# Two-layer transformer block, one core: one order of products for the gated layer, its last rows stored by tiles, up biases prepared by VectorE, and stage exits without a barrier where there is nothing to clear

## The reference, cut to what matters

```python
xn = layernorm(x)
x1 = x + attention(xn) + experts(xn)          # layer 0
zn = layernorm(x1)
out = x1 + lightning(zn) + gated(zn)          # layer 1

def experts(x):                               # two experts, every token takes one
    e0 = argmax(softmax(x @ Wg.T)) == 0
    out0 = gelu(x @ W0a.T + b0a) @ W0b.T + b0b
    out1 = relu(x @ W1a.T + b1a) @ W1b.T + b1b
    return where(e0, out0, out1)

def gated(x):                                 # ternary weights q(w), hidden width 1408
    return (sigmoid(x @ q(w1).T) * (x @ q(w2).T)) @ q(w3).T
```

## Time and profile before

| | us |
|---|---|
| three executions | 1728.63, 1733.5, 1733.7 |
| the profiled execution's own time | 1733.02 |
| its span, first to last instruction | 1731.2 |
| expert stage, first SyncE issue to the last add | 888.01 to 1122.3 |
| gated stage, first matmul to the end of the span | 1476.76 to 1731.2 |
| mean granted TensorE clock, share of full | 0.955 |

### The profile page before, as it was taken

How to read it: one execution, slowest core, us unless ns; L and a number is a source line. 1 busy time by engine, 2 the same in 40 slices (tenths; PEclk the granted TensorE clock), 3 DMA queues, 4 the chain that set the end, 5 groups by cost and what they waited for, 6 DMA issues and landing times. The chain is left out here.

```text
span 1731.2 us, 22070 instructions
## 1 busy us (share of the span) xinstructions
PE 1556.5 (90%) x7890; PEld 1080.1 (62%) x7890; DVE 989.4 (57%) x1698; ACT 603.2 (35%) x1137; POOL 647.9 (37%) x530
## 2 busy tenths in 40 slices
PE   5998769999999999996979999839999996999997
PEld 4886434444545555543757777737777774788886
DVE  7764857778877888762435555445654445222232
ACT  3221225555555555554212122144424222222221
POOL 4000033376788677784336666523120201000000
PEclk9998879999999999998989999959999997999999
DMA  6876503645545375224741211153030105320210
GB/s 229 264 232 205 118 4 86 128 104 103 129 119 113 78 180 116 57 87 132 242 140 55 67 56 58 52 186 128 1 122 1 50 31 152 116 98 1 98 49 25
DMA packets 103257, 182.28 MB, mean 105 GB/s; under 512 B 29018, under 2 KB 45290, under 8 KB 101274
## 3 DMA queue, kind: packets, MB, share of 16 engines
q1 hardware_dynamic: 85636, 121.39, 25.6%
q0 software_dynamic: 13648, 51.61, 10.0%
q10 hardware_dynamic: 3866, 7.87, 1.4%
HBM read 118.83 MB, written 62.02 MB: 104 GB/s over the span
## 5 line engine op out<-in xcount | busy, mean ns | idle before, releaser
L999 ACT ACTIVATE att_probs<-att_ring 128x512 f32<-128x512 f32 (+3 forms) x640 | 298.8, 537 | 295.5 <-DVE att_ring L1036 154.5
L1027 DVE TENSOR_REDUCE att_maxes<-att_ring 128x2 f32<-128x1024 f32 (+7 forms) x366 | 338.7, 946 | 68.2 <-PE att_ring L921 58.0
L956 PE MATMUL att_outp<-att_probs,att_vs 128*64 128x512 f32 (+3 forms) x1280 | 276.1, 553 | 0.3 <-ACT att_att L982 0.3
L956 PEld LDWEIGHTS att_outp<-att_probs,att_vs 128*64 128x64 f32 x1280 | 79.6, 139 | 122.0 <-issue 70.8
L942 PE MATMUL att_ring<-route_wah,route_wbh 102*128 102x512 f32 (+2 forms) x320 | 106.1, 408 | 13.4 <-ACT att_probs L999 7.3
L921 PE MATMUL att_ring<-route_wbh,route_wah 100*128 100x512 f32 (+2 forms) x320 | 103.8, 406 | 14.7 <-PEq L57 6.4
L921 PE MATMUL att_ring<-moew_wbl,moew_wal 100*128 100x512 f32 (+2 forms) x320 | 98.7, 384 | 17.2 <-ACT att_probs L999 9.0
L1685 DVE TENSOR_TENSOR glu_hid<-glu_sig,glu_u 128x512 f32<-128x512 f32 x44 | 30.2, 687 | 139.0 <-ACT glu_sig L1663 139.0
L1700 POOL DMA_DIRECT2D out<-glu_y x4 | 3.1, 787 | 278.2 <-DVE glu_y L1691 278.2
L942 PEld LDWEIGHTS att_ring<-route_wah,route_wbh 102*128 102x128 f32 x320 | 55.5, 194 | 76.1 <-issue 44.3
L942 PE MATMUL att_ring<-moew_wal,moew_wbl 102*128 102x512 f32 (+2 forms) x320 | 100.4, 399 | 2.4 <-DVE att_maxes L1027 2.3
(11 more groups left out here) (270 smaller groups left out, 3516.0 us busy)
## 6 DMA issues: line engine op xcount, KB each, us to landing
att_q_raw<-in_w POOLq DMA_DIRECT2D x48, 352.0 KB, 4.1
w_ternary<-att_q_out POOLq DMA_DIRECT2D x24, 352.0 KB, 2.7
tail_up<-w_ternary SPq DMA_DIRECT2D x22, 256.0 KB, 4.9
xn<-qkv_x SPq DMA_DIRECT2D x4, 1024.0 KB, 7.8
q_hi<-qkv_hi SPq DMA_DIRECT2D x16, 256.0 KB, 3.9
q_lo<-qkv_lo SPq DMA_DIRECT2D x16, 256.0 KB, 4.5
k_hi<-qkv_hi SPq DMA_DIRECT2D x16, 256.0 KB, 2.9
k_lo<-qkv_lo SPq DMA_DIRECT2D x16, 256.0 KB, 3.9
```

Source lines behind the costliest of these rows:

```text
L956: last = pe.matmul(outp[v_cols(h), off:CH], vs[p % 2][:, kt, v_cols(h)], probs[:, g % 4, h, off:CH], start=kt == 0, stop=kt == TT * (c + 1 ...
L999: act.activation(probs[:, g % 4, h, off:CH], ring[:, rg.banks["score", g][h], off:CH], ACT.Exp).then_inc(exped, 1)
L1027: last = dve.tensor_reduce(maxes[:, hs, t, g:g + 1], banks[:, :, 0:width], AX.X, ALU.max)
```

## The change

Four edits. An exit without semaphores neither clears nor waits at a barrier, and `up_in` moves from `Kept` into the `lin` stage, where SyncE waits for it as its last act; so `tail` has no semaphore either. In the expert stage `ba` has a semaphore of its own and VectorE subtracts in it; GpSimd waits for the other two tables and keeps their two operations. In the gated stage the loops over chunk and step become one loop over 44 steps, so that the first two up products of a chunk stand between the last down products of the one before; the sigmoid waits for `u1_made`, signalled behind the eighth matmul; VectorE's chunk-end add comes one step into the next chunk. In the last down product each token tile signals by itself, VectorE adds it (128x512) and SyncE stores it (256 KB).

```diff
@@ class Stage
     def __exit__(self, *a):
         self.stack.__exit__(*a)
-        self.nc.clear_and_free_semaphores(self.sems)
-        self.nc.all_engine_barrier()
+        if self.sems:
+            self.nc.clear_and_free_semaphores(self.sems)
+            self.nc.all_engine_barrier()
@@ experts_stage, SyncE
-            for dst, src in ((ba, ba_d), (bb, bb_d), (bo, bo_d)):
+            sp.dma_start(ba[:], ba_d).then_inc(ba_in, 16)
+            for dst, src in ((bb, bb_d), (bo, bo_d)):
                 sp.dma_start(dst[:], src).then_inc(b_in, 16)
@@ experts_stage, VectorE
             x_low(0)
-            dve.wait_ge(b_ready, 3)
+            dve.wait_ge(ba_in, 16)
+            dve.tensor_tensor(ba[:, 0, :], ba[:, 0, :], ba[:, 1, :], ALU.subtract).then_inc(ba_ready, 1)
+            dve.wait_ge(ba_ready, 1)
             select(0)
...
                 mix(0, half)
+            dve.wait_ge(b_ready, 2)
             down_bias(0)
@@ experts_stage, GpSimd
-            pool.wait_ge(b_in, 3 * 16)
-            for t in (ba, bb):
-                pool.tensor_tensor(t[:, 0, :], t[:, 0, :], t[:, 1, :], ALU.subtract).then_inc(b_ready, 1)
-            pool.wait_ge(b_ready, 2)
+            pool.wait_ge(b_in, 2 * 16)
+            pool.tensor_tensor(bb[:, 0, :], bb[:, 0, :], bb[:, 1, :], ALU.subtract).then_inc(b_ready, 1)
+            pool.wait_ge(b_ready, 1)
             pool.tensor_tensor(bb[:, 1, :], bb[:, 1, :], bo[:], ALU.add).then_inc(b_ready, 1)
@@ lightning_stage, SyncE
             for f in range(GT):
-                kept.load(sp, up_d, f)
+                kept.load(sp, up_d, f, up_in)
             sp.wait_ge(z_stored, (NCH - 1) * 32)
+            sp.wait_ge(up_in, GT * 32)
@@ glu_stage, SyncE, behind its loop
+            for t in range(TT):
+                sp.wait_ge(tile_added, t + 1)
+                sp.dma_start(rows_of(out_d, GLU_CHUNKS[NCH - 1])[:, t, :], y[:, t, :]).then_inc(tile_stored, 16)
+            sp.wait_ge(tile_stored, TT * 16)
@@ glu_stage, TensorE (the loop before is in the listing above)
+            def up_product(n):
+                c, f = divmod(n, GT)
+                if f == 0 and c:
+                    pe.wait_ge(x_in[c % 2], (c + 1) // 2 * 32)
+                pe.wait_ge(hid_ready, n + 1)
+                for w, u, made in ((w1, u1, u1_made), (w2, u2, upped)):
...
+                    last.then_inc(made, 1)
+
+            def down_product(n):
+                c, f = divmod(n, GT)
+                if f == 0:
+                    pe.wait_ge(added, c + 1)
+                if c == 0:
                     pe.wait_ge(down_in[load_of[f]], 16)
+                pe.wait_ge(lo_ready, n + 3)
+                for t in range(TT):
...
+                    if n == NF - 1:
+                        last.then_inc(tile_made, 1)
+                if n < NF - 1:
                     last.then_inc(downed, 1)
+            up_product(0)
+            up_product(1)
+            for n in range(NF):
+                down_product(n)
+                if n + 2 < NF:
+                    up_product(n + 2)
@@ glu_stage, ScalarE
+            for n in range(NF):
+                act.wait_ge(u1_made, n + 1)
+                act.wait_ge(hid_ready, n + 1)
+                act.activation(sig[:, n % 2, :], u1[:, n % 2, :], ACT.Sigmoid).then_inc(sig_ready, 1)
+                act.wait_ge(hid_ready, n + 3)
+                act.wait_ge(downed, n - 1 + LEAD)
+                act.activation(hh[:, n % 2, :], hid[:, n % 2, :], ACT.Copy).then_inc(hi_ready, 1)
@@ glu_stage, VectorE
+            def finish(c):
+                dve.wait_ge(y_free, c + 1)
+                if c:
+                    dve.wait_ge(r_in, c * 16)
+                if c + 1 < NCH:
+                    dve.wait_ge(downed, c * GT + GT + LEAD)
+                    dve.tensor_tensor(y[:], resid[:], down[:], ALU.add).then_inc(added, 1)
...
+                for t in range(TT):
+                    dve.wait_ge(tile_made, t + 1)
+                    dve.tensor_tensor(y[:, t, :], resid[:, t, :], down[:, t, :], ALU.add).then_inc(tile_added, 1)
...
+            for n in range(NF):
+                dve.wait_ge(upped, n + 1)
+                dve.wait_ge(sig_ready, n + 1)
...
+                if n and n % GT == 0:
+                    finish(n // GT - 1)
+            finish(NCH - 1)
@@ glu_stage, GpSimd
-            for c in range(NCH):
+            for c in range(NCH - 1):
```

More of the change, by code:

```diff
@@ L1300, in experts_stage @@
         up, down = st.ps("up", [P, 2, CH]), st.ps("down", [P, 2, D])
-        b_in, b_ready = st.sem("b_in"), st.sem("b_ready")
+        ba_in, b_in, ba_ready, b_ready = (st.sem(n) for n in ("ba_in", "b_in", "ba_ready", "b_ready"))
         gathered, fetched, stored = ([st.sem(f"{n}{i}") for i in range(k)]
@@ L1545, in __init__ @@
         self.up = [st.sb(f"up{i}", [P, GT, KT, P], F32R) for i in range(2)]
-        self.up_in = st.sem("up_in")
         self.xh, self.xl = st.sb("xh", [P, KT, CH], F32R), st.sb("xl", [P, KT, CH], F32R)
@@ L1558, in spare, with load @@
         return self.up[i][:, 2 * KT + j]
-    def load(self, eng, w_d, f):
+    def load(self, eng, w_d, f, arrived):
         for w, src in zip(self.up, w_d):
             eng.dma_start(w[:, f].bitcast(F32), src[:, f * P:(f + 1) * P].rearrange("(k p) n -> p k n", p=P)
-                          ).then_inc(self.up_in, 16)
+                          ).then_inc(arrived, 16)
 GLU_CHUNKS = [NCH - 1] + list(range(NCH - 1))
@@ L1584, in glu_stage @@
         x_in, r_in = [st.sem(f"x_in{i}") for i in range(2)], st.sem("r_in")
-        upped, sig_ready, hid_ready = st.sem("upped"), st.sem("sig_ready"), st.sem("hid_ready")
+        u1_made, upped, sig_ready, hid_ready = (st.sem(n) for n in ("u1_made", "upped", "sig_ready", "hid_ready"))
         hi_ready, lo_ready, downed = st.sem("hi_ready"), st.sem("lo_ready"), st.sem("downed")
+        tile_made, tile_added, tile_stored = st.sem("tile_made"), st.sem("tile_added"), st.sem("tile_stored")
         added, y_ready, stored, y_free = st.sem("added"), st.sem("y_ready"), st.sem("stored"), st.sem("y_free")
         block = st.block()
-        LEAD = 2 * GT
+        LEAD, NF = 2 * GT, NCH * GT
         def load_down(eng, i):
@@ L1614, in _ @@
             pe.sem_inc(downed, LEAD)
-            for c in range(NCH):
[L1616 to L1629, removed]
-                    pe.wait_ge(down_in[load_of[f]], 16)
[L1631 to L1635, removed]
-                    last.then_inc(downed, 1)
[L1638 to L1646, removed]
@@ new lines, in up_product @@
+            def up_product(n):
[4 more added lines that the diff above has]
+                for w, u, made in ((w1, u1, u1_made), (w2, u2, upped)):
+                    for k in range(KT):
+                        pe.matmul(u[:, n % 2, :], w[:, f, k, :], xh[c % 2][:, k, :], start=k == 0, stop=False)
+                        last = pe.matmul(u[:, n % 2, :], w[:, f, k, :], xl[c % 2][:, k, :], start=False, stop=k == KT - 1)
+                    last.then_inc(made, 1)
@@ new lines, in down_product @@
+            def down_product(n):
[3 more added lines that the diff above has]
+                if c == 0:
+                    pe.wait_ge(down_in[load_of[f]], 16)
+                pe.wait_ge(lo_ready, n + 3)
+                for t in range(TT):
+                    s = slice(t * P, (t + 1) * P)
+                    pe.matmul(down[:, t, :], hh[:, n % 2, s], w3[:, f, :], start=f == 0, stop=False)
+                    last = pe.matmul(down[:, t, :], hl[:, n % 2, s], w3[:, f, :], start=False, stop=f == GT - 1)
+                    if n == NF - 1:
+                        last.then_inc(tile_made, 1)
+                if n < NF - 1:
+                    last.then_inc(downed, 1)
@@ L1666, in _ @@
         @block.vector
         def _(dve):
+            def finish(c):
[5 more added lines that the diff above has]
+                    dve.tensor_tensor(y[:], resid[:], down[:], ALU.add).then_inc(added, 1)
+                    dve.wait_ge(added, c + 2)
+                    dve.sem_inc(y_ready, 1)
+                    return
+                for t in range(TT):
+                    dve.wait_ge(tile_made, t + 1)
+                    dve.tensor_tensor(y[:, t, :], resid[:, t, :], down[:, t, :], ALU.add).then_inc(tile_added, 1)
@@ L1671, in _ @@
             dve.sem_inc(y_ready, 1)
[L1672 to L1693, removed]
+            for n in range(NF):
+                dve.wait_ge(upped, n + 1)
+                dve.wait_ge(sig_ready, n + 1)
+                dve.wait_ge(lo_ready, n + 1)
+                dve.tensor_tensor(hid[:, n % 2, :], sig[:, n % 2, :], u2[:, n % 2, :], ALU.mult).then_inc(hid_ready, 1)
+                dve.wait_ge(hi_ready, n + 1)
+                dve.tensor_tensor(hl[:, n % 2, :], hid[:, n % 2, :], hh[:, n % 2, :].bitcast(F32),
+                                  ALU.subtract).then_inc(lo_ready, 1)
+                if n and n % GT == 0:
+                    finish(n // GT - 1)
+            finish(NCH - 1)
         @block.gpsimd
```

(2 more changed lines are left out.)

## The result

The changed kernel takes 1722.9 us (median of five, 1714.9 to 1725.8) against 1733.7 (median of five, 1728.6 to 1736.9): ratio 0.9921, 95% interval 0.9898 to 0.9944, so it is faster, by 0.6 to 1.0%. The forecast was 1721.3. The profiled execution took 1725.83 us with a span of 1724.0.

The account below looks back on a forecast made before the run. TensorE, busy 90% of the span, was taken as the bound, leaving gaps, clock and stage ends. Terms 4.0 + 4.2 + 1.3 + 2.4 = 11.9 off 1733.02 gave 1721.1, forecast as 1721.3 after splitting the offset to the median; range 1717.0 to 1726.5.

Parts of the forecast that it names:

- Chunk ends: Gated stage: next chunk's up products cover TensorE's wait and restart at three boundaries of 1.33 us, -4.0 us.
- The end: After the last up product: sigmoid off the path 0.63, tile adds 0.84, SyncE's tile stores 2.3, exit 0.4; together -4.2 us.
- Barriers: Stage exits: three empty barriers after the experts at 0.3 us each and one at the end at 0.4; -1.3 us.
- Experts: Opening of the expert stage: GpSimd loses its 2.40 us bias subtraction, so ReLU and second `mix` come earlier; -2.4 us.
- the third: Rival: experts' opening gives 4.5 us instead of 2.4, clock staying full after a shorter gap, ReLU faster; 1719.0, chance 0.08.
- the fourth rival: Slower: TensorE's clock stays at half in the experts' first tiles, 12 us a tile; 1739 at one and a half, chance 0.03.
- The first rival: Small terms pay half: last stores queue, giving back 2.1 us, and the experts' opening gives 0.5; 1725.1, chance 0.13.

Follow-up runs that it names:

- bias_only: Kernel before with only the `ba` semaphore and VectorE's bias subtraction added; it took 3.1 us off the experts.
- order_only: Kernel before with only the single order of products, sigmoid still behind the whole up product; gated stage 237.2 us against 241.2.
- add_twice: Changed kernel with the chunk-end add of 128x2048 done twice; gated stage 4.7 us more than 237.2.
- one_store: Changed kernel with the four tile adds but one 1 MB store by SyncE; landing 4.3 us, end 11.2 us long against 9.1 to 9.2.
- select_late: Changed kernel with `select(1)` moved behind the two mixes; expert stage 1.2 us longer, longest ReLU 2.02 us in place of 3.0.
- bb_on_vector: Changed kernel with both operations on `bb` moved from GpSimd to VectorE; 1716.7 us, ratio 0.9903 to the kernel before.

## Why the prediction was right

- **The sum, -11.9**: at equal clock the touched stretches gave -13.5 to -13.7. In the profile the gated stage's opening at half clock took 1.6 of it back, which nobody had forecast. That the sum was met to the tenth is luck; the mechanisms are shown one by one, each at its term or a little over it.
- **Chunk ends, -4.0**: measured -4.0 with the clock alike on both sides. The profile's -2.4 is this less the half-clock opening.
- **The end, -4.2 and 0.4 for its barrier**: measured -5.6. Gate signal -0.7 (0.6 forecast). From the last down product's start to the last add's end 3.4 us (3.7), since the four adds took 2.48 together where 2.82 was reckoned. Store 2.3 from add to landing (2.7). The exit from landing to the last instruction 0.9 (1.1), 1.1 less than before. Each term a little too careful, all the same way.
- **Barriers, -0.9 after the experts**: -1.0. The moved wait for the weights cost nothing visible: of lightning's 1.1 us more, 0.7 and 0.9 also stand in bias_only (346.1) and order_only (346.3), which have it not, while add_twice and one_store have it and took 344.3. TensorE's gap ahead of the gated stage is 2.0 us with it and 2.1 to 2.3 without.
- **Experts, -2.4**: -2.9 to -3.1. The path was named rightly; the size of one thing on it was not. The prediction let the two gathers keep their length, but the first took 0.96 us instead of 2.00, since it no longer began under `select(0)`, while the `bb` subtraction, now beside `select(0)`, took 1.71 in place of 1.29: 2.4 + 1.04 - 0.42 = 3.0. Those 0.4 and the ReLU's 3.00 us beside a `select` against 2.02 without are what the Trainium skill, GPSIMD Engine Reference, Key points, says of VectorE instructions with two SBUF inputs: the traces agree with it. The prediction's own estimate by it, 0.7 us lost on the subtraction and 0.5 won on the ReLU, came out as 0.4 and nothing, and it had left out the gather, the largest case.
- **Rivals**: the clock did stay at full after the gap of 1.5 us, as the third had it (the matmul at 903.43 took 0.49, not 0.79), but of its 2.1 beyond the forecast only 0.5 to 0.7 came, and by the gather, not by the clock: the ReLU held TensorE back. Behind the first 6 us of the stage TensorE kept the full clock, also behind the gaps of 1.71 and 0.96 us, so the fourth rival did not come; select_late shows that its danger was real. The first rival's slow store did not come: the last landed within 2.3.
- **The range**: its lower bound of the gain, about -6, is not the sum of the terms' own bounds, which give -2.5 (1730.5). With them the range would have reached past 1728.3, under which alone the prediction counts the kernel as faster.

## What to carry to other kernels

Read an in-order stage's boundaries as a pipeline that drains: the gain of running over them is the wait plus the restart, and it holds as long as what is put in between is longer than the chunk-end work beside it; test that by doubling the latter. When an engine's wait goes, look at what the next wait on it hangs on before counting the whole, and look which instructions of a second engine will now begin under a long one of the first. Where executions spread by more than a part is worth, cut the profiles at the same events and compare stretches with equal granted clock.

## What the runs showed that I had not expected

The same instructions ahead of the expert stage took from 880.6 to 891.6 us in these profiles, more than the whole gain of any part; their mean clock was 0.95 to 0.96, and why they differ is open. And GpSimd's drain at the experts' exit, here in the changed kernel, stands behind a store that has already landed:

```profile
L55 POOLq DRAIN  x1: 4050/4050/4050, 1126.2 to 1126.2; - x1
```

At the gated stage's exit it was 0.38; what makes the difference is not shown. Leaving it out took 4.1 us off that exit, and nobody waited for it later: lightning took 346.1 us against 345.8 in the profile of the timed bb_on_vector.
